# Dense stages of a recurrent kernel on scaled fp16 pairs, with scales exchanged through DRAM, and x W placed by one operation

## The reference

```
c = layernorm(cond) * gamma + beta;  h = gelu(c @ W1 + bias1);  a1, b1, a2, b2 = split(h @ W2 + bias2)
u   = x . a2[b]                                 # (B,T,R)
mid = gelu(x @ base_down + u . b2[b])           # (B,T,D)
v   = mid . b1[b]
x1  = 2x + mid @ base_up.T + v . a1[b]          # first layer and its residual
xW  = x1 @ Wx + bias;  h_t = tanh(xW_t + h_(t-1) @ Wh);  y = x1 + h
```

## Time and profile before

| | |
|---|---|
| median of runs | 1219.49 us |
| profiled execution: time / span | 1219.28 / 1217.2 us |
| TensorE busy | 1189.4 us (98%) |
| VectorE / ScalarE / GpSimd busy | 893.3 / 640.5 / 254.6 us |
| from the span's start to the first recurrent step | about 135.7 us |
| a steady chunk of 32 steps | 67.9 us |

### The profile page before, as it was taken

The page is one execution under the profiler, slowest core; times in us unless marked ns, Lnnn a source line. Parts: engine busy times, 40 slices in busy tenths (PEclk is TensorE's granted clock), DMA queues, the critical chain, the costliest instruction groups (busy, mean ns, idle before and its releaser), DMA issues.

```text
span 1217.2 us, 50835 instructions
## 1 busy us (share of the span) xinstructions
PE 1189.4 (98%) x21046; PEld 959.8 (79%) x21046; DVE 893.3 (73%) x3648; ACT 640.5 (53%) x2648; POOL 254.6 (21%) x523
## 2 busy tenths in 40 slices
PE   8977999999999999999999999999999999999998
PEld 7544888888888888888888888888888888888755
DVE  4433577887877787887877777878778777877676
ACT  4121455656555655656555655656555556555443
POOL 0000122222222222222222222222222222222221
PEclk8888999999999999999999999999999999999999
DMA  9899211312221221312221221212121211102021
GB/s 316 314 397 324 36 20 21 54 21 37 36 36 23 37 38 20 55 20 41 34 37 23 38 34 29 46 20 49 26 38 31 35 29 31 27 3 37 2 46 28
DMA packets 260565, 75.73 MB, mean 62 GB/s; under 512 B 247952, under 2 KB 248096, under 8 KB 260336
## 3 DMA queue, kind: packets, MB, share of 16 engines
q1 hardware_dynamic: 258112, 72.35, 25.2%
q10 hardware_dynamic: 2224, 0.14, 0.2%
HBM read 55.68 MB, written 16.78 MB: 60 GB/s over the span
## 4 chain that ended last, share of the span: by engine, by line
PE 92%; DMA 4%; ACT 1%; DVE 1%; issue 1%; SPq 0%; POOLq 0%; POOL 0%
PE bulk L1075 47%; PE rec L1091 34%; PE bulk L1078 5%; DMA work<-in_L_cond_W_dram 4%; PE bulk L1064 2%; PE bulk L1053 2%; ACT rec L599 1%; DVE z L925 1%; PE rec L978 0%; PE bulk L1237 0%; PE bulk L1204 0%; SPq L486 0%; PE rec L1075 0%; PE bulk L1019 0%; ACT gel L639 0%
## 5 line engine op out<-in xcount | busy, mean ns | idle before, releaser
L1091 PEld LDWEIGHTS rec<-hs,wh_s 128*128 128x128 f16 x16352 | 443.4, 96 | 134.1 <-DVE hs L933 124.0
L1091 PE MATMUL rec<-hs,wh_s 128*128 128x32 f16 x16352 | 492.8, 177 | 6.2 <-ACT rec L599 6.2
L679 ACT ACTIVATE hf<-z 128x32 f32<-128x32 f32 x1024 | 232.6, 230 | 435.5 <-DVE z L925 399.4
L556 POOL TENSOR_TENSOR work<-work,hf 128x64 f32<-128x64 f32 x512 | 253.2, 495 | 957.8 <-DVE hs L933 956.8
L925 DVE TENSOR_REDUCE z<-rec 128x32 f32<-128x96 f32 x1022 | 262.8, 257 | 190.6 <-PE rec L1091 165.4
L1075 PE MATMUL bulk<-mid_s,up_s 128*128 128x512 f32 x768 | 222.9, 410 | 0.6 <-ACT mid_s L640 0.5
L933 DVE SCALAR_TENSOR_TENSOR hs<-hf,hs 128x32 f16<-128x32 f32 x1022 | 196.6, 192 | 35.2
L1075 PE MATMUL bulk<-act_x,down_s 128*128 128x512 f32 x768 | 219.9, 410 | 0.0
L1075 PE MATMUL bulk<-act_s,wx_s 128*128 128x512 f32 x756 | 208.4, 408 | 0.0
L930 DVE TENSOR_SCALAR hs<-hf 128x32 f16<-128x32 f32 x1022 | 181.4, 178 | 6.3 <-ACT hf L679 4.9
L599 ACT ACTIVATE rec<-work 128x32 f32<-128x32 f32 x1022 | 184.9, 213 | 0.0
(11 more groups left out here) (129 smaller groups left out, 681.2 us busy)
## 6 DMA issues: line engine op xcount, KB each, us to landing
work<-in_L_cond_W_dram SPq DMA_DIRECT2D x33, 1024.0 KB, 8.1
out_dram<-work SPq DMA_DIRECT2D x240, 64.0 KB, 2.5
work<-in_x_dram SPq DMA_DIRECT2D x224, 64.0 KB, 3.9
work<-in_x_dram SPq DMA_DIRECT2D x8, 256.0 KB, 9.7
work<-in_L_cond_base_up_dram SPq DMA_DIRECT2D x1, 1024.0 KB, 8.1
work<-in_L_cond_base_down_dram SPq DMA_DIRECT2D x1, 1024.0 KB, 12.9
wh_f<-in_L_cond_Wh_dram SPq DMA_DIRECT2D x1, 1024.0 KB, 16.5
wh_f<-in_L_cond_Wx_dram SPq DMA_DIRECT2D x1, 1024.0 KB, 5.4
```

The lines of the kernel that those rows point to most:

```text
L556: nc.gpsimd.tensor_tensor(to, xs, hf[:, t % 4], ALU.add).then_inc(sum_done, 1)
L679: nc.scalar.activation(hf[:, t % 4, half], z[:, half], ACT.Tanh, scale=inv_reg).then_inc(tanh_done, 1)
L1091: last = nc.tensor.matmul(R[fo][:, m, 0:PARTS, :], wh_s[:, q, k, n * P:(n + 1) * P], hs[:, k, :, :], start=(m == k == q == 0), stop=(k == ...
```

## The change

From chunk 3 on (`F16_FROM = 3`) the dense stages' operands are pairs of fp16 numbers, scaled by powers of two, in place of pairs of fp32r numbers; the passes and the number of matmuls stay. The low-rank matmuls and u, v stay as they are. In detail:

* The weights: seven maxima of weights and factors are taken in the start (six) and in step 1 (one) by VectorE reduces over 512 to 2048 elements, sent through DRAM to every partition, reduced again in step 8 (896 elements), and turned into scales by 14 small GpSimd operations. From step 42 ScalarE rescales one 512-column piece of weights a step (36 steps), and GpSimd does 24 operations of 512 columns (steps 45 to 79) to make the fp16 pairs.
* The data: for each chunk three bounds (of x, of mid, of x1), from ScalarE sums of magnitudes (`Abs` with `accum_out`: four of x, four of gelu's result, one each of the two rank values), combined by GpSimd, and made the same on all partitions by an exchange: SyncE writes 128 numbers to DRAM, waits, reads them back broadcast to all partitions. VectorE waits for the broadcast, reduces 128 numbers and masks the exponent; GpSimd makes the scales.

| bound | GpSimd combines in slot | VectorE waits for the broadcast in slot |
|---|---|---|
| x | -16 (step 16 of the chunk before last) | -12 (step 20) |
| mid | -1 (step 31) | 3 |
| x1 | 11 | 15 |

* Slots move: x is turned in slots -31, -30, -19, -18 (before -19, -18, -8, -7), its high parts are made in -10, -9, -6, -4, its low parts in -8, -7, -5, -3; x1 gets a fourth buffer; y is turned in slots 3, 4, 5, 8. Gelu runs once, and a scaled copy in slots 5, 6, 8, 9 takes the place of the second. x1 is no longer doubled by VectorE but by GpSimd, eight operations of 256 columns in slots 24 to 31.
* ScalarE's operations on these data take their scale from a per-partition pointer operand.
* `place` writes x W of a step by one operation; the first quadrant waits for all of it.

```diff
-            for c in range(2, 4):
-                next_x(c)
-            for c in range(NC - 1):
-                store_y(c, range(P // SQ))
-                if c + 4 < NC:
-                    next_x(c + 4)
...
+            def exchange(n, i, ready, mine, gone, every, back):
+                count = n - F16_FROM + 1
+                sp.wait_ge(ready, count)
+                if count > 1:
+                    sp.wait_ge(back, 16 * (count - 1))
+                sp.dma_start(tops[i].rearrange("(p o) -> p o", o=1), mine).then_inc(gone, 16)
+                sp.wait_ge(gone, 16 * count)
+                sp.dma_start(every, tops[i:i + 1].broadcast_to([P, P])).then_inc(back, 16)
+            for c in range(NC):
+                main, ahead = F16_FROM <= c + 1 < NC, F16_FROM <= c + 2 < NC
+                if main:
+                    exchange(c + 1, 0, u_topped, ur[:, 0:1], u_out, u_all[:], u_back)
+                if c >= 1:
+                    store_y(c - 1, range(P // SQ))
+                if main:
+                    exchange(c + 1, 1, g_topped, gr[:, 0:1], g_out, g_all[:], g_back)
+                if 4 <= c + 3 < NC:
+                    next_x(c + 3)
+                if ahead:
+                    exchange(c + 2, 2, x_topped, xr[:, 0:1], x_out, x_all[:], x_back)
...
+                j = r - DOUBLE_AT
+                if 0 <= j < 2 * KT:
+                    if j == 0:
+                        pool.wait_ge(x1lo_done, (n + 1) * KT)
+                    part = x1[n % 4][:, j // 2, j % 2 * (COLS // 2):(j % 2 + 1) * (COLS // 2)]
+                    nc.gpsimd.tensor_tensor(part, part, part, ALU.add).then_inc(doubled, 1)
...
-            def place(n, f):
+            def place(n):
...
-                nc.scalar.activation(R[f][:, :, PARTS, :],
-                                     xw[:, c % 2].rearrange("p k (b t) -> p k b t", t=TC)[:, f * HT:(f + 1) * HT, :, t],
+                nc.scalar.activation(RX, xw[:, c % 2].rearrange("p (f m) (b t) -> p f m b t", f=2, t=TC)[:, :, :, :, t],
                                      ACT.Copy).then_inc(xw_placed, 1)
...
+                for k in tile_at(at["xsum"], r):
+                    act.wait_ge(x_tr, n * KT + k + 1)
+                    need(act, xsum_done, (n - F16_FROM) * KT + k)
+                    nc.scalar.activation(x_junk[:], x1[n % 4][:, k], ACT.Abs, accum_out=xsum[:, k:k + 1]).then_inc(xsum_done, 1)
...
+                if n >= F16_FROM and r == XSCALE_AT:
+                    dve.wait_ge(x_back, 16 * (n - F16_FROM + 1))
+                    link(nc.vector.tensor_reduce(xr[:, 1:2], x_all[:], AX.X, ALU.max))
+                    power(xr[:, 2:3], xr[:, 1:2]).then_inc(x_powered, 1)
...
-                    dense(mid, i, at["mid_banks"], down_s, act_x, b2_s, mid_mm)
+                    dense(mid, i, at["mid_banks"], *((down_s, act_x) if n < F16_FROM else (down16, x16)), b2_s, mid_mm)
```

More of the change, by code:

```diff
@@ L124 @@
 Y_SLOT = (3, 4, 7, 9)
+F16_FROM = 3
+F16_TOP = 2.0 ** 14
+LEAST = 2.0 ** -60
+XT16_AT, XT16_FIRST = (-31, -30, -19, -18), (-21, -20, -19, -18)
+XSUM_AT, XSUM_FIRST = (-30, -29, -18, -17), (-19, -18, -17, -16)
+XTOP_AT, XSCALE_AT = -16, -12
+UTOP_AT, USCALE_AT = -1, 3
+GTOP_AT, GSCALE_AT = 11, 15
+GHI_AT, MLO_AT = (5, 6, 8, 9), (6, 7, 9, 10)
+Y16_SLOT = (3, 4, 5, 8)
+W_SCALE_AT = 8
+XHI16_AT = (-10, -9, -6, -4)
+XLO16_AT = (-8, -7, -5, -3)
+GSUM_AT = (6, 8, 10, 11)
+X1HI16_AT = (17, 18, 19, 22)
+DOUBLE_AT = 24
+TOPS_AT = (11, 13, 23, 12, 28, 20)
+CONVERT_AT = (F16_FROM - 2) * 32 + 10
 STREAM = 40
@@ L543, in _, with link, inverse @@
                                         pattern=[[RANK, GB]], channel_multiplier=-1).then_inc(pool_set, 1)
+            nc.gpsimd.memset(expo[:], float("inf"))
+            nc.gpsimd.memset(turn_bits[:], 2.0 ** 127).then_inc(pool_set, 1)
+            pool.wait_ge(pool_set, 8)
+            links = [0]
+            def link(ins):
+                links[0] += 1
+                ins.then_inc(pchain, 1)
+                pool.wait_ge(pchain, links[0])
+            def inverse(out, src):
+                n = src.shape[1]
+                link(nc.gpsimd.tensor_tensor(out.bitcast(U32), turn_bits[:, 0:n].bitcast(U32), src.bitcast(U32), ALU.subtract))
@@ new lines, in other @@
+            def other(n, r):
+                if n < F16_FROM:
+                    return
+                if r == XTOP_AT:
+                    x_top(n)
+                if r == XSCALE_AT:
+                    x_scales(n)
+                if r == UTOP_AT:
+                    mid_top(n)
+                if r == USCALE_AT:
+                    mid_scales(n)
+                if r == GTOP_AT:
+                    state_top(n)
+                if r == GSCALE_AT:
+                    state_scales(n)
+                j = r - DOUBLE_AT
[4 more added lines that the diff above has]
+                    nc.gpsimd.tensor_tensor(part, part, part, ALU.add).then_inc(doubled, 1)
@@ L556, in _ @@
                     nc.gpsimd.tensor_tensor(to, xs, hf[:, t % 4], ALU.add).then_inc(sum_done, 1)
+                    if n == W_SCALE_AT:
+                        weight_scales()
+                    for j in range(24):
+                        if n == CONVERT_AT + 3 + j // 2 * 3 + j % 2:
+                            convert(j)
+                    if c + 1 < NC:
+                        other(c + 1, t)
+                    if c + 2 < NC:
+                        other(c + 2, t - TC)
         @block.scalar
@@ L679, in chunk @@
                         nc.scalar.activation(hf[:, t % 4, half], z[:, half], ACT.Tanh, scale=inv_reg).then_inc(tanh_done, 1)
-                    for f in range(2) if n + 1 < T else ():
-                        place(n + 1, f)
+                    if n + 1 < T:
+                        place(n + 1)
                     if c + 1 < NC:
@@ L911, in _ @@
                     split_weight(1, wx_f, wx_s)
+                for j in tile_at(TOPS_AT, i):
+                    top_of(j)
                 dense_slot(0, i)
@@ L1152, in dense_slot @@
                         pe.wait_ge(fac_split, KT + m + 1)
-                    dense(out, i, at["out_banks"], up_s, mid_s, a1_s, out_mm)
+                    dense(out, i, at["out_banks"], *((up_s, mid_s) if n < F16_FROM else (up16, g16)), a1_s, out_mm)
                 for i in xw_plan[1].get(r, ()):
```

309 lines of the change are left out of this document (283 added, 26 removed).

## The result

The changed kernel takes **1502.92 us** (median of four runs, 1500.74 to 1505.7) against 1219.17 in the same comparison: ratio 1.2335, 95% interval 1.2306 to 1.2365, 284 us slower. The prediction was 1213, and the time is far outside its range. The side is that of case C, with a price several times its own.

A forecast was written before the change was run, and what follows sets the result against it. TensorE, busy 98% of the span, was taken to bound the kernel, above a recurrence floor of about 1.8 us a step. 1219.3 - 41 (chunks) + 21 (x's exchange) + 11 (rescaling) + 3 (maxima) = 1213 us, range 1189 to 1233.

The forecast's parts named there:

- case C: Rival: a small transfer takes 3.2 us, not 2.1; x1's exchange stalls 1.3, x's comes later; 1240 us; chance 0.15.
- my own formula: Exchanges: GpSimd's finish plus two transfers of 2.1; x1 lands 8.2 against 9.0, mid 7.1 against 8.7, both free.
- x's exchange behind the loads: SyncE's queue: x's small write waits behind 16 loads; VectorE waits 1.9 us in slot 20, 11 times, 21 us lost.
- TensorE and the fp16 operands: Dense slots: fp16 matmuls at 0.215 us each; five-matmul step 1.875 from 2.06; TensorE's work falls 4.9 us a chunk.
- Case E: Rival: fp16 matmuls no faster than fp32r, steps stay at 2.06, only losses left; about 1245 us; chance 0.05.
- VectorE's slots: Slots 3, 15, 20: added reduce, wait and tiny operation, 0.45 us, make steps of 2.27; loss 0.8 us a chunk.
- ScalarE: Sums of magnitudes at 0.6 us fit; gelu then scaled copy in slot 9 delays tanh; loss 0.3 a chunk.
- GpSimd's lock: VectorE and GpSimd exclude each other; doublings in slots 24, 25, 27, 29 delay splits; 0.5 us a chunk (0 to 1.3).
- case D: Rival: GpSimd's lock also stops the first split, or its operations reach their upper bounds; 1232 us; chance 0.12.
- A chunk: Steady dense chunk: 67.9 - 4.9 + 0.8 + 0.3 + 0.6 = 64.7 us; 3.2 less, 13 times, 41 us gained.
- the 1.8 us floor: Recurrence latency (reduce, tanh, two splits): no dense step can fall under about 1.8 us.
- Once: One-time costs: rescaling in steps 42 to 79, 11 us lost (5 to 20); seven weight maxima, 3 lost (0 to 6).

## Why the prediction was wrong, step by step

**The step that failed** is "The nearest small one lands in 1.8 us, a 64 KB store in 2.4; I take 2.1 for each with SyncE's wake-up". Bytes were the wrong likeness: the earlier trace rows shows no transfer whose pieces are 4 bytes side by side in DRAM. Measured: 7.8 us and 5.5 in mid's exchange, 9.4 and 4.8 in x's. Put into my own formula, mid's bound lands at 2.9 + 7.8 + 5.5 = 16.2 us against 8.7, 7.5 late, and the wait is 5.0 by the trace; for x1's it gives 3.9 + 7.5 + 4.4 = 15.8 against 9.0, 6.8 late, and the wait is 6.2. So the formula, with the right prices, is too long by 2.5 and 0.6 us, and finds both stalls; with 2.1 it found none. The form of the sum was sound and the price was not. The bounds I gave it came only from transfers that seemed alike; and that case C decides from 2.4 us on should have told me that the forecast hung on a duration which no row showed.

**x's exchange behind the loads** was the right place, and too small at the right transfer price as well. With spaced numbers and the order unchanged the kernel takes 1243.5, with the order changed too 1181.0: 62 us, where I had 21 and 41 as upper bound. Of these 47 are in slot 20, 4.3 us a chunk where I had 1.9, and 14 in slots 22 and 23, at the lower clock. The write behind the loads was right (3.5 against 3.7). The loads were not: I took 0.53 us an issue, the low end, and 16 take 11.7 us and not 8.5; even my high end, 0.64, gives 10.2. The read takes 2.8 and not 2.1.

**The lower clock after a wait** was in no term of the sum, and no reason was given for leaving it out. It is most of the 48 us in the steps behind the waits. Whether the forecast's own stall of 1.9 us would have brought it is not shown; the nearest case is chunk 2 of the kernel with 512 bytes between the pieces, where slot 20 is 2.1 us too long and slots 22 and 23 keep their 1.85 and 2.01 us.

**TensorE and the fp16 operands**: right (1.88 us for five matmuls; predicted 1.875). Case E is refuted.

**VectorE's slots**: right. Without exchanges the steps of slots 3, 15, 20 take 2.14, 2.29 and 2.25 us; predicted 2.27.

**ScalarE**: slot 10 lost 0.42 us for 0.3. The sum of magnitudes is two instructions, not one; the groups of the kernel without exchanges, by form:

```profile
L883 ACT ACTIVATE g_junk<-gel 128x512 f16<-128x512 f32 x44 | 27.0, 615 | 0.0
L883 ACT ACTIVATION_READ_ACCUMULATOR g_junk<-gel 128x1 f32 x44 | 8.2, 188 | 0.0
```

So 0.80 us and not 0.6. The steps that hold it are not longer for it.

**GpSimd's lock**: the direction that the earlier trace rows could not show does exist. The timeline of the same kernel: a doubling on GpSimd, and VectorE's rounding of the state, which otherwise takes 0.18 us.

```profile
657.59 0.61 POOL L789 TENSOR_TENSOR work<-work 128x256 f32<-128x256 f32 x1
...
657.91 0.32 DVE L1301 TENSOR_SCALAR hs<-hf 128x32 f16<-128x32 f32 x1
```

It ends where the doubling ends, 658.2. It happens once in each of chunks 3 to 14, twelve times. The Trainium skill (SBUF — State Buffer, Who interferes with whom) says that the engine that begins first keeps the shared pair for its whole instruction; this row agrees. The split with two SBUF operands, which the prediction named, was never held from 400 to 1100 us (0.19 us each of 702). What was held is the first of the two operations, near what case D named (the lock "also stops the first split"). But a doubling takes 0.61 us (I took 0.75), and where it held the rounding the step had slack: I charged 0.5 us a chunk, and the doubling slots stay at 2.10 and 1.88 us, nothing. Case D's mechanism exists, and its price is refuted.

**A chunk** without exchanges: 63.7 us, 64.7 by my sum. Half of the difference is the doublings. Some 0.4 more is given back in slots 16 and 21, right behind steps that VectorE made longer: they take 1.73 and 1.85 us, where the fp16 matmuls alone would give 1.87 and 2.13. So a step that VectorE lengthens is in part paid back by the next (from reduce to reduce), which the sum left out, and the 1.8 us floor that I drew does not hold for such a step.

**Once**: without exchanges, rescaling cost about 8.5 us (chunk 1 and 2 against the steady gain) where I took 11; chunk 0 lost 5.8 where I took 3. In the kernel after, 5.0 of its 6.3 are the wait for the weights' maxima; taken up in step 20 in place of 8, chunk 0 loses 1.0. **The place** cost 1.8 to 2.0 us where I took nothing.

**The rivals.** Case C named the mechanism (the transfers' price, stalls at x1, then x) and the point at which it decides; its 3.2 us was too small by more than four for the write and by one to two for the read. It also left mid's exchange free, though its own price puts mid's bound at 2.9 + 6.4 = 9.3 us against 8.7; that exchange stalls 5.0 us a chunk.

**Left open.** What happens between the last record of a packed write and its landing, and why the broadcast read's first data come 1.7 us later after such a write (that both wait for the same memory is my guess; nothing shows it). From which distance below 64 bytes pieces hold each other up. Whether the instruction loads that coincide with the long steps of slot 2 are their cause.

## What to carry to other kernels

A transfer's price follows its pieces, where they land and what is queued ahead of it, not its bytes: where a trace has no transfer of the same shape and the sum turns on it, the range must be as wide as that ignorance, or the transfer is measured alone first. Put a small transfer that an engine waits for ahead of bulk loads on its queue. To bring one number per partition to all of them, three times a chunk, a transpose, a reduce and a matmul with ones made a chunk 1.5 us longer here, and exchanges through DRAM with packed 4-byte pieces 20 us by waiting and some 5 more in slow steps. The exchange through DRAM was made free too, by spacing the pieces and issuing ahead of the loads, but only in a kernel that reads constants back.

## What the runs showed of the hardware that was not expected

* 128 pieces of 4 bytes from 128 partitions into 512 contiguous bytes of DRAM: 7.0 to 7.7 us in the median with no loads ahead. The same pieces 64 or 512 bytes apart: 1.4. One piece of 512 bytes from one partition: 1.1. The packed pieces' records are over 1.0 us after the issue, as the spaced ones' are; the rest is between the last record and the landing. The Trainium skill (DMA: Bandwidth & Descriptors, Specifications) says that the DMA engines do read-modify-write for transfers under 512 bytes. That rule does not tell neighbours from pieces that are apart; here 4-byte pieces cost 1.4 against 1.1 us when they are apart, and the large price comes only when they are neighbours. Whether read-modify-write is behind it no run shows.
* A 64 KB broadcast read of those 512 bytes takes 2.8 to 3.1 us in the median, and 4.1 to 4.9 when they have just been written packed. 16 KB instruction loads that overlap a packed write take 2.9 us in the median, others 1.1. A small write behind 16 queued loads of 64 KB takes 3.3 to 3.5 us in place of 1.4.
* After TensorE had stood still for 5.92 us the granted clock was 0.50 (1.2 GHz) for 1.9 us and 0.54 for the next 2.9, and a step of 1.9 us took 2.9. Over the kernel after, the mean clock is 0.898; without exchanges it is 0.985.
* Sixteen load issues of 64 KB take SyncE 11.6 to 13.5 us, 0.73 to 0.85 each.
